# A planner's table of durations replaced by measured ones, and its choice among ready pieces replaced by the longest path of work to the end

## The reference, cut to what matters

```python
x = x + attn_a(_layernorm(x), ...)      # q, k, v; sums over shifted k and v with softmaxed gains; gate; out
x = x + ffn(_layernorm(x), ...)         # top-1 of 8 experts: 128 -> 512 gelu -> 128
x = x + attn_b(_layernorm(x), ...)      # a recurrence along the 512 steps, and a norm
x = x + ffn(_layernorm(x), ...)         # the same experts again

# attn_a
for j in range(N_SCALES):               # 11 scales, shifts d * tau < 512
    for tau, h_coef in enumerate(D4):
        qk = jnp.sum(q * k_s, axis=-1, keepdims=True)
        out = out + g_j * h_coef * qk * v_s
return gathered * gate @ W_out.T + b_out

# attn_b
def step(h, xb_t):
    h = jnp.tanh(h @ A.T + xb_t)
    return (h, h @ C.T)
```

## Time and profile before

| | us |
|---|---|
| median of three runs | 1432.24 |
| lowest and highest | 1431.16, 1438.38 |
| span of the profiled execution | 1436.4 |
| PE busy (share) | 1170.8 (82%) |
| DVE, POOL, ACT busy | 796.3, 788.6, 651.3 |
| first and last tanh of the recurrence | 446.5, 1262.0 |

### The profile page before, as it was taken

One profiled execution on the slowest core, in us unless ns is written; L12 is line 12 of the kernel. 1 busy time (PEld: TensorE's weight loads), 2 busy tenths in 40 slices (PEclk: granted clock), 3 DMA queues, 4 the chain that ended last, 5 costly groups with the idle time before them and its releaser, 6 DMA issues. The chain is left out here.

```text
span 1436.4 us, 32831 instructions
## 1 busy us (share of the span) xinstructions
PE 1170.8 (82%) x9942; PEld 881.1 (61%) x9942; DVE 796.3 (55%) x1723; ACT 651.3 (45%) x2050; POOL 788.6 (55%) x1274
## 2 busy tenths in 40 slices
PE   3877886888888899789988899887899998995580
PEld 2644554566565666466655666676787777785570
DVE  4878788889966777576788647542122301240110
ACT  2233332465544664455554436363564344562250
POOL 2645458563776748862748844876315642324504
PEclk9989987999988998889999759788995567998895
DMA  4700001221221212111112221233332324444542
GB/s 126 213 1 0 1 1 47 61 65 58 86 66 44 64 44 70 51 51 38 44 46 86 60 63 46 77 97 105 108 104 77 98 83 123 118 132 121 146 116 60
DMA packets 117638, 107.58 MB, mean 75 GB/s; under 512 B 15540, under 2 KB 88541, under 8 KB 117469
## 3 DMA queue, kind: packets, MB, share of 16 engines
q1 hardware_dynamic: 106704, 88.01, 21.5%
q0 software_dynamic: 8192, 16.79, 3.9%
q10 hardware_dynamic: 2573, 0.69, 0.2%
HBM read 76.73 MB, written 28.70 MB: 73 GB/s over the span
## 5 line engine op out<-in xcount | busy, mean ns | idle before, releaser
L799 POOL TENSOR_TENSOR acc<-acc,term 128x512 f32<-128x512 f32 x219 | 281.5, 1286 | 71.9 <-DVE term L1341 54.8
L1160 PE MATMUL bank<-w,hT 128*128 x1088 | 217.5, 324 | 22.1 <-ACT hT L985 13.9
L1341 DVE TENSOR_TENSOR term<-bank,V 128x512 f32<-128x512 f32 x251 | 168.0, 684 | 67.2 <-PE bank L1110 44.0
L1005 ACT ACTIVATE hid<-bank 128x16 f32<-128x16 f32 x512 | 93.0, 182 | 243.6 <-PE bank L1187 203.0
L985 ACT ACTIVATE hT<-bank,b1T 128x128 f32<-128x128 f32 x544 | 165.2, 370 | 79.2 <-PE bank L1147 65.2
L839 POOL DMA_INDIRECT back<-sorted_y,slot_i x128 | 125.1, 978 | 135.8 <-DMA back<-sorted_y,slot_i 44.2
L1160 PEld LDWEIGHTS bank<-w,hT 128*128 128x128 f32 x1088 | 173.9, 221 | 41.1 <-issue 35.6
L1187 PEld LDWEIGHTS bank<-hid,abcT 128*32 128x32 f32 x4096 | 88.6, 116 | 162.2 <-ACT hid L1005 83.2
L1312 DVE SCALAR_TENSOR_TENSOR made<-bank,qkvb,K 128x512 f32<-128x512 f32 x251 | 176.2, 742 | 17.8 <-PE bank L1083 7.2
L1187 PE MATMUL bank<-hid,abcT 128*32 128x16 f32 x4096 | 138.6, 201 | 38.3 <-ACT hid L1005 37.1
L1147 PE MATMUL bank<-xTb,w1b 128*128 128x128 f32 x864 | 166.8, 321 | 3.2 <-ACT xTb L973 3.0
(11 more groups left out here) (177 smaller groups left out, 2153.4 us busy)
## 6 DMA issues: line engine op xcount, KB each, us to landing
w1b<-in_W SPq DMA_DIRECT2D x130, 256.0 KB
K<-in_W SPq DMA_DIRECT2D x54, 256.0 KB
xsb<-sorted_x SPq DMA_DIRECT2D x184, 64.0 KB
sorted_y<-ysb SPq DMA_DIRECT2D x136, 64.0 KB
X<-in_x SPq DMA_DIRECT2D x64, 64.0 KB
out_x<-X SPq DMA_DIRECT2D x64, 64.0 KB
sorted_x<-K SPq DMA_DIRECT2D x14, 256.0 KB, 3.6
sorted_y<-made SPq DMA_DIRECT2D x48, 64.0 KB
```

The lines of the kernel that those rows point to most:

```text
L799: nc.gpsimd.tensor_tensor(acc[:], acc[:] if k > 1 else term[0][:], term[k % NTERM][:], ALU.add).then_inc(S["terms_added"], 1)
L1005: nc.scalar.activation(hid[n % 2][:, cs], bank[6 + n % 2][:, cs], ACT.Tanh).then_inc(S["h_ready"], 1)
L1160: last = nc.tensor.matmul(bank[SLOT_BANK[place(n)]][:, 0:D], tile(hT[place(n)], c), w2[:, ds(second[n] + c * D, D)], start=(c == 0), stop= ...
L1341: V_.tensor_tensor(term[k % NTERM][:], bank[2 + k % 2][:], V[:, at:at + CW], ALU.mult).then_inc(S["terms_ready"], 1)
```

## The change

The planned duration of each piece was one number, written beside the piece; now it is two, `pace` (how long its engine is held) and `took` (how long until its result is there), from one table, with a further table of delays from engine to engine. Engines get begin times, a change of ACT's function table between `exp` and `gelu` is counted, and a piece that follows another of its kind on one engine says so. Before planning, `to_go` is worked out for every piece: the longest sum of durations from it to the end of the program. Of the pieces of an engine that are ready within 0.15 us of the earliest, the one with the largest `to_go` is taken. `URGENT` is gone. Nothing that is computed changes, nor any wait between pieces, buffer or ring; only each engine's order does, and with it the matmuls of `fillings()` (730 in 132 places instead of 486 in 83).

```diff
-    def piece(engine, what, n, k, us, rank, after, lands=0.15, bank0=None):
-        us = us * PE_PACE if engine == "PE" else us
-        todo[what, n, k] = [engine, us, rank, [x for x in after if x is not None], lands, bank0]
+Piece = namedtuple("Piece", "engine pace took after bank0")
...
+    exp=(0.70, 0.79), high=(0.65, 0.63), kcopy=(0.58, 0.67), vcopy=(0.58, 0.67), pcopy=(0.49, 0.60), pnorm=(0.38, 0.48),
...
+    loadw=(1.10, 3.75), loadx=(0.45, 2.25), store=(0.45, 2.25), outst=(0.62, 2.60))
...
+LANDS = {"scatter": 1.75, "gather": 1.70}
+BEGINS = {"PE": 23.5, "ACT": 23.5, "DVE": 22.5, "POOL": 12.0, "SP": 22.0}
+TABLE_US, TURN_US, LOOK_US, DAWDLE = 1.283, 0.11, 0.15, 50.0
...
-        piece("ACT", "exp", i, 0, 3.3, USUAL, [("shift", i, 1)])
+        piece("ACT", "exp", i, 0, [("shift", i, 1)])
...
-                    piece("SP", "outst", CHUNK_OF_PREP[p], k, 0.1, rank, [("gadd", p, 0)])
+                    piece("SP", "outst", CHUNK_OF_PREP[p], k, [("gadd", p, 0)])
...
-        piece("SP", "loadw", s, 0, 0.3, rank,
-              [("texp", n, 0), past("loadw", s - 1)]
-              + ([LAST_READS[0]] if 0 <= late < LATE_RING else [past("hidden", s - ring, parts(s - ring) - 1)]), lands=3.2)
+        piece("SP", "loadw", s, 0, [("texp", n, 0), past("loadw", s - 1)]
+              + ([LAST_READS[0]] if 0 <= late < LATE_RING else [past("hidden", s - ring, parts(s - ring) - 1)]))
...
-            piece("PE", "step", c, k, 0.28, URGENT,
-                  [("state", c, k - 1) if k else past("state", c - 1, CT - 1), ("rxb", c, 0) if k == 0 else None])
+            piece("PE", "step", c, k, [("state", c, k - 1) if k else past("state", c - 1, CT - 1), ("rxb", c, 0) if k == 0 else None])
...
+    while ends:
+        key = ends.pop()
+        to_go[key] = max((hop(todo, key, y) + to_go[y] for y in followers[key]), default=todo[key].took)
...
-                choice = (at, todo[key][2], ready, key)
-                if pick is None or choice[0] < pick[0] - 1e-9 or (abs(choice[0] - pick[0]) < 1e-9 and choice[1:3] < pick[1:3]):
-                    pick = choice
...
+            if r <= now + LOOK_US:
+                choice = (DAWDLE * max(0.0, r - now) - to_go[key], key)
+                if best is None or choice < best[0]:
+                    best = choice, max(r, now)
```

More of the change, by code:

```diff
@@ new lines, in cost @@
+def cost(what, n, k):
+    if what in ("hidden", "result"):
+        us = 0.222 * HC / parts(n)
+        return us, us + 0.17
+    if what == "gelu":
+        us = 0.25 * HC / parts(n)
+        return us, us + 0.12
+    if what == "spread" and terms(n)[k].g not in (0, 1):
+        return 0.87, 1.02
+    if what == "spread":
+        return 0.31, 0.47
+    if what == "scale" and k == 2:
+        return 0.21, 0.31
+    if what == "xmom" and STATS_GROUP[n][1] - STATS_GROUP[n][0] == 1:
+        return 3.16, 3.17
+    return PACE[what]
@@ L192, in past, with pieces, piece @@
+def pieces():
+    todo = {}
+    def piece(engine, what, n, k, after, bank0=None):
+        todo[what, n, k] = Piece(engine, *cost(what, n, k), [x for x in after if x is not None], bank0)
     def past(what, n, k=0):
         return (what, n, k) if n >= 0 else None
-    URGENT, USUAL = 0.0, 1.0
     for i in range(CHUNKS):
@@ L327, in timeline @@
         x = JOB[n]
-        rank = USUAL
         prev = past("turn", s - 1)
@@ new lines, in pieces @@
+            piece("ACT", "gelu", s, h, [("hidden", s, last), past("result", prior(s), parts(prior(s)) - 1), ("gelu", s, h - 1) if h else None])
+            piece("PE", "result", s, h, [("gelu", s, last), ("result", s, h - 1) if h else None])
+        piece("DVE", "yadd", s, 0, [("result", s, last), past("store", prior(s))])
+        piece("SP", "store", s, 0, [("yadd", s, 0), past("store", s - 1),
+                                               ("gadd", CHUNKS_BEFORE[n - 1] - 1, 0) if n >= 2 else None])
@@ L376, in timeline @@
-    engines = ["SP", "POOL", "ACT", "PE", "DVE"]
-    left = {key: len(x[3]) for key, x in todo.items()}
+            piece("PE", "step", c, k, [("state", c, k - 1) if k else past("state", c - 1, CT - 1), ("rxb", c, 0) if k == 0 else None])
+            piece("ACT", "state", c, k, [("step", c, k), past("ry", c - 2) if k == 0 else None])
+        piece("PE", "ry", c, 0, [("state", c, CT - 1)])
+        piece("DVE", "rres", c, 0, [("ry", c, 0)])
+        piece("DVE", "rstats2", c, 0, [("rres", c, 0), past("rmom2", c - 2)])
@@ new lines, in pieces, with hop @@
+        piece("POOL", "rmom2", c, 0, [("rstats2", c, 0), past("rnorm2", c - 2, TPC - 1)])
+        for k in range(TPC):
+            piece("ACT", "rnorm2", c, k, [("rmom2", c, 0), ("rnorm2", c, k - 1) if k else None])
+        piece("DVE", "rgam", c, 0, [("rnorm2", c, TPC - 1)])
+        piece("DVE", "rbeta", c, 0, [("rgam", c, 0)])
+        piece("DVE", "rout", c, 0, [("rbeta", c, 0)])
+    return todo
+def hop(todo, x, y):
+    e, f = todo[x].engine, todo[y].engine
+    return todo[x].took + HOP_OF.get((x[0], y[0]), HOP.get((e, f), 0.08)) + LANDS.get(x[0], 0.0)
@@ L438, in fillings @@
         for b, last in reader.items():
-            since = max(end, BEGIN[last] + WORK[last][1] + FREE_US) if last else end
+            since = max(end, BEGIN[last] + WORK[last].took + FREE_US) if last else end
             if best is None or since < best[0]:
```

250 lines of the change are left out of this document (122 added, 128 removed).

## The result

The changed kernel takes 1472.6 us (median of four runs, 1471.2 to 1489.0) against 1434.2 us (four runs of the kernel before, one more than in the table ahead): a ratio of 1.032, 95% interval [1.024, 1.040]. It is slower by 3%; the forecast was 1390 us, and its range ended at 1446. In three later sessions, on two chips, it took 1486.7, 1489.9 and 1483.1 us, ratios 1.029, 1.038 and 1.039. The loss is firm. Its cause is only partly settled, as the experiments show.

A forecast was written before the change was run, and what follows sets the result against it. PE's work and rate bound the middle, chains the first and last stretches. The terms -8 + 131 - 144 - 20 + 24 - 25 = -42 on 1436.4 gave 1394, at the median 1390 us; range 1350 to 1446.

The forecast's parts named there:

- Part 1: Up to the first step (446.5 us): five slots move behind it, -8 us, bounds -30 and +15.
- Part 2: Chunks 0 to 5 (262.5 us): 115 us of PE work moved in, at 1.138 us each, +131 us.
- prediction's own sign: End of the recurrence: the prediction is wrong if the last step comes after 1275.
- Parts 3, 4 and 5: Chunks 6 to 15 (553 us): work moved out -144, fewer holes -20, lower clock +24, leaving 413 us.
- Part 4: Two holes without steps in chunks 6 to 15: PE idle share falls from 13% to 7%, -20 us.
- part 5: Clock in chunks 6 to 15: thinner work between steps raises the share at half clock from 0.38 to 0.50, +24 us.
- third rival: Chunks 6 to 15: without holes the clock stays up, stretch 328 us, 1305 us at the median; chance 0.05.
- Part 6: After the last step (174.4 us): job 7's slots run closer, store first and output writes behind loads, -25 us.
- The first: Rival: thin work keeps chunks 6 to 15 at half clock, stretch 474 us, 1451 us at the median; chance 0.18.
- It doesn't do what it says: Rival, whole kernel: unforeseen new waits eat parts 4 and 6, moved work gains nothing, about 1432 us; chance 0.13.

The follow-up runs named there:

- experiment 5: Changed kernel, but gathers and what else leads up to a chunk's steps go first when ready, steps and tanhs don't: 1454.6 us, 1.019 of before.
- experiment 4: Changed kernel, but an engine with a step or state update ready takes it (steps first): 1320.7 us, 0.927 of before; again 1471.9 us, 1.023.
- experiment 6: Kernel before, with each output write placed behind the last store: 1421.6 us, 0.999 of before.

## Why the prediction was wrong

**Part 1** held: -6 for -8. 560 filling matmuls instead of 417 did not make the first step later.

**Part 2 is the step that failed.** Its form was work times one rate. The work was mis-sized: 146.6 us for 115, 36 us of the miss at 1.138. With each matmul counted up to the start of the next at most, slots make about 78 us of the work (67 forecast, their 1.98 us being more like 2.3 there), mixer chunks 53 (48 forecast), router passes and job preparation 14 and the steps' own matmuls 4, both forecast at nothing. The granted clock, 0.88 for 0.91, is part of each. The rate makes the other half: 377.2 x (1.22 - 1.138) is 31 us. 1.138 came from a stretch in which a ready step won every tie. With steps behind everything that has a longer path, PE's idle grew from 29 to 71 us, and in experiment 5, without pauses, the stretch takes 446.5 us as well. I wrote down that `URGENT` was gone and never gave it a price. The sentence that DVE "has room" was true (294 of 460 us) and beside the point: what counted was the order within an engine, not how full it was. Chunk 6, forecast near 832, began at 900.8, and the last step, which by the prediction's own sign should come before 1275, at 1310.

**Parts 3, 4 and 5 together** held, 409.3 us for 413, and in part by luck. Part 4's gain did not come: it wanted PE's idle share down from 13% to 7%, and it was 11.6% before (64.1 of 553) and 11.7% after (47.7 of 409.3). Two holes are left, 41 us before chunk 12 and 24 before chunk 14, where 128 us stood. The clock fell further than part 5 took, to 0.71 for 0.75, a share at half clock of 0.58 for 0.50; by its own formula that alone makes 430 us. Both misses go one way, so parts 3 or 5 had an error the other way that no run takes apart. PE's work without filling matmuls fell by 124.6 us, and at the old rate of 1.152 that is the whole change of 144.

Part 5's mechanism, thin work that holds the clock down, is not shown as the cause of the 0.71. In the traces without unnamed waits the same chunks have 0.88 (experiment 5) and 0.90 (4), and steps first has 0.90 without pauses and 0.76 with them, from the same instructions. What does hold is that a busy PE is no promise either way: as in the earlier trace rows, experiment 6 stays at 0.50 from 1060 to 1100 us with PE recorded busy throughout, and experiment 4 at 1.00 from 901 to 997 us with PE busy for 94.7 of 96 (all engines, columns as above):

```profile
1060.00:1100.00 40.00, 40.00 (x338) 32.55 (x337) 14.89 (x48) 17.20 (x66) 23.95 (x48) 0.50 0.28 79
```

```profile
901.00:997.00 96.00, 94.73 (x1438) 74.64 (x1438) 35.64 (x126) 65.52 (x270) 67.90 (x175) 1.00 0.32 92
```

The third rival, for which the clock stays up once the holes are gone, did not come true in the changed kernel. The Trainium skill (TensorE: Matmul & The Clock Gate, "HAM oscillation") lays the fall on waits between groups of matmuls. The fall from 0.90 to 0.76 with the pauses agrees with it; that the clock stays at 0.50 through 40 us of a busy PE is not explained by such waits.

**Part 6** was half right. From the first load to the end of the last `yadd` the slots take 59.8 us (1370.91 to 1430.72) instead of 80.3, for 53 forecast; the prediction had written 78 for the 80.3, a slip of subtraction. The first `yadd` follows the load by 10.9 us instead of 15.7 (4.8 gained for 6), and the 22 intervals behind it are 2.2 us each, not 1.98. Of these 20.5 us the ends gave back 6.4: the first load stands 60.8 us behind the last step (57.4 before), and 39.8 us follow the last `yadd` (36.8). Experiment 6 adds that the output writes, which the prediction named first, were worth nothing by themselves.

**The rivals.** The first had the right sign with the wrong mechanism: it put the loss into chunks 6 to 15 at half clock, which came out at 409 us, not 474. "It doesn't do what it says" named the failure in general (new waits by pieces in order) and gave it no place and a price of zero. A rival "the recurrence waits behind other work in chunks 0 to 5" was missing. The prediction mentions up to 52 pieces between two steps in chunks 1 and 2, and prices none; from the order alone 473 pieces of PE stand between the steps of chunks 0 to 5 where 285 stood, and that could have been counted before. And the range took no account of how much two executions of one program may differ: 105 and 153 us, in two versions that run PE tighter than the kernel before does.

## What to carry to other kernels

When a planner drops a priority for a recurrence, count on each engine what stands between two of its links, and give that a price; the longest path alone doesn't know that every engine will be late. Without pauses better durations were worth 6.5% in one session, more than the rule that used them cost. And don't compare two versions across sessions by their ratios to a common baseline: put both into one session, since the baseline may move by 1% where another version moves by 11%.

## What the runs showed of the hardware

- One program took 1317 to 1346 us in one session and 1467 to 1489 in another, and a second one 1343 to 1350 and 1434 to 1459, the kernel before 1426 and 1441 (medians). In the last session the kernel before took 1427 us while the changed kernel's trace had unnamed waits, so the time of the baseline does not tell which kind of session it is.
- In the slower sessions the distance from one matmul of PE to the next is often 1 to 8 us longer, 37 times in one pair of traces of one program and 31 in another (5 and 8 times the other way round). 33 and 25 of them overlap an indirect DMA on POOL, but so do 14 of the 19 longer distances of experiment 6, which has no unnamed wait. The cause is open.
- The Trainium skill (Perfetto Trace Analysis, "DMA Instruction — SWDGE (GPSIMD)") says that the recorded end of such an instruction is when the last of GpSimd's processors has written its descriptors, and not when the data have moved. No run here shows that this delays PE.
- PE's clock is lower there: 0.92 over the whole span becomes 0.86 with the same instructions.
- With the filling matmuls the clock up to the first step is 0.96, without them 0.80; the kernels differ by 24 us, in two sessions without unnamed waits.
- PE can be recorded busy for 40 us without a break and stay at half clock (experiment 6), and for 94.7 of 96 us at full clock (experiment 4).
